# The first two bf16 parts of the second batch's keys: cast on GpSimd instead of ScalarE

## The chip, the cores and the metric

The kernel runs on one core of one Trainium2 chip. The metric is the device time of one execution in microseconds. The core has TensorE (matrix products, written to PSUM), VectorE, ScalarE and GpSimd (elementwise work), and SyncE, on whose queue this kernel issues all its DMAs. The engines run on their own and meet at semaphores only.

## The reference, cut to what matters

The whole reference is two layers of three blocks each (attention over a context, a state-space scan, a low-rank mixture; attention over the context with a mask, attention with compressed and local keys, a mixture of 8 experts), on x of shape (2, 128, 256). The change lies in the first block, and in the work of its second batch:

```
x = x + mha(layernorm(x), ctx, ctx)         # x (2, 128, 256), ctx (2, 2048, 256), 16 heads of 16
scores = einsum('bhqd,bhkd->bhqk', qh, kh) / sqrt(16)
scores = where(ki <= qi + (2048 - 128), scores, -10000)
out = einsum('bhqk,bhkd->bhqd', softmax(scores), vh)
```

Keys and values are the same f32 context. The kernel computes the scores in bf16 with enough parts to come near f32: each key is split into three bf16 parts, part 1 = bf16(K), residue = K - part 1, part 2 = bf16(residue), part 3 = residue - part 2.

## The kernel before, in words

**Groups.** The first block is cut into 8 groups of 4 heads: groups 0 to 3 are batch 0, groups 4 to 7 batch 1. The keys of a group lie in `kS[g % 3]`, 6 x 16 rows of parts (query part times key part) and 2 rows of ones. SyncE fills them with 12 DMAs a group (line 287) out of `ks3[b][part]`, the parts of all keys of batch b. For a group of batch 1 it waits first until `k1_done`, `k2_done` and `k3_done` stand at 6, and before every group from 3 on until the group that used the buffer is over (`pv_done`).

**Passes.** In pass g (g = 0 to 7) two things run beside each other. First, group g is weighed: in 16 chunks of 128 keys TensorE makes the scores plus the bias -max (line 917), ScalarE takes their exponential (line 679), TensorE multiplies by the values (line 930). There are two PSUM buffers of scores, so the scores of chunk c + 2 wait for the exponential of chunk c. Second, TensorE makes the scores of group g + 1 once more (lines 886 to 890), and VectorE reduces them to the maxima of each row in 8 pieces (line 1677). Four tiny VectorE operations behind the eighth (lines 1683 to 1688, semaphore `nm_done`) make the bias of the next group from them: the bias chain. TensorE turns it into rows (line 900), ScalarE copies these (line 579), and the next pass may start. The maxima of group 0 are made ahead of pass 0; `nm_done` stands at g + 2 when the bias chain of pass g is done.

**What ScalarE does beside it.** Other steps are put into ScalarE's order by hand, in the table `beside`: the key (g, c) says that a step runs ahead of the exponential of chunk c in pass g. Among them are `late_part1(j)` and `late_part2(j)` for the 4 heads j of the second batch's K, each one cast of 128x1024, f32 to bf16, and `late_query_rows` (passes 1 and 2), copies of the second batch's queries from PSUM.

**What GpSimd does beside it.** It runs through the groups in order: for each it copies the values into `va[g % 2]` (line 449, semaphore `va_ready`, needed by the first product of values of pass g). For g = 1 it then waits until `nm_done` is 2 (end of pass 0) and makes the residues of the second batch (`late_residue`, line 411, in place in `ctxK`); for g = 2 it waits until `nm_done` is 3 (end of pass 1) and makes part 3 (`late_part3`, line 417). For g = 6 it makes 16 products for the state-space block (lines 437, 425), which begin in pass 5.

**Queries.** `split_queries(1)` on VectorE (lines 1404 to 1408, semaphore `q_split`) splits the queries of the second batch right behind the bias chain of group 0, ahead of the reductions of pass 0.

Of the kernel before, what the change touches and what calls it, by code (L numbers as in the profile page):

```python
# [26 lines left out]
HPG = 4  # L27
# [33 lines left out]
def view(region, start, words, dtype=F32):  # L61
    part = region[:, start:start + words]
    return part if dtype == F32 else part.bitcast(dtype)


def perceiver_program(nc, io, out):
    ctx = ExitStack()
    sems = {}
    with ctx:
# [3 lines left out]
        def S(name):  # L73
            if name not in sems:
                sems[name] = ctx.enter_context(nc.semaphore(name))
            return sems[name]
# [13 lines left out]
        ctxK = reg_a[:, 0:8192].rearrange("p (b j k) -> p b j k", b=NB, j=HPG)  # L90

        part_at = [((reg_b, 12288), (reg_b, 14336), (reg_b, 16384)), ((reg_a, 0), (reg_a, 2048), (reg_b, 18432))]
        ks3 = [[view(r, a, 2048, BF16).rearrange("p (j k) -> p j k", j=HPG) for r, a in ats] for ats in part_at]
# [25 lines left out]
        def weights_of(region, at, gap):  # L119
# [8 lines left out]
               for r, at in ((part_b, 4096), (part_a, 0))]  # L128
# [36 lines left out]
        q_split = [view(oreg, 1024 * b, 768, BF16).rearrange("p (h d t) -> p h t d", h=H0, t=PARTS)  # L165
                   for b in range(NB)]
# [226 lines left out]
        def _(pool):  # L393
            def inv_sqrt(t, b):
                pool.wait_ge(S(f"ln_var{b}"), t + 1)
                pool.tensor_tensor(rstd[b][:, :], var_eps[b][:, :], neg_half, ALU.pow).then_inc(S(f"ln_rstd{b}"), 1)  # L396
# [9 lines left out]
            for i in range(2):  # L406
                pool.wait_ge(S("cleared"), 2)
                pool.memset(va[i][:, :, :, HD0:HD0 + 1], 1.0).then_inc(S("ones_set"), 1)
            def late_residue(j):
                pool.wait_ge(S("k1_done"), 2 + j + 1)  # L410
                pool.tensor_tensor(ctxK[:, 1, j, :], ctxK[:, 1, j, :], ks3[1][0][:, j, :], ALU.subtract)\
                    .then_inc(S("kres_done"), 1)

            def late_part3(j):
                pool.wait_ge(S("kres_done"), 2 + j + 1)
                pool.wait_ge(S("k2_done"), 2 + j + 1)
                pool.tensor_tensor(ks3[1][2][:, j, :], ctxK[:, 1, j, :], ks3[1][1][:, j, :], ALU.subtract)\
                    .then_inc(S("k3_done"), 1)

            def state_input(h):  # L420

                pool.wait_ge(S("dtx_done"), 1)
                pool.wait_ge(S("b_in"), 16)
                for n in range(0, NS, 4):
                    pool.tensor_tensor(state[0][:, h, n:n + 4],
                                       tmp[0][:, h * P:(h + 1) * P].unsqueeze(1).to_broadcast([P, 4, P]),
                                       bc_row[0][:, n:n + 4, :], ALU.mult).then_inc(S("dbx_done"), 1)

            def decay_exponent(h):

                pool.wait_ge(S("ea_done"), 1)
                pool.wait_ge(S("kS_in1"), 16 * REP * 3)
                pool.wait_ge(S("dtx_done"), 1)
                for n in range(0, NS, 4):
                    if (h, n) == (0, 12):
                        pool.wait_ge(S("nm_done"), 6)
                    pool.tensor_tensor(decay[0][:, h, n:n + 4],
                                       dt[0][:, P * h:P * (h + 1)].unsqueeze(1).to_broadcast([P, 4, P]),
                                       ea[:, h, n:n + 4].unsqueeze(2).to_broadcast([P, 4, P]), ALU.mult)\
                        .then_inc(S("dta_done"), 1)  # L440


            for g in range(NG):
                b, hg = divmod(g, NHG)
                pool.wait_ge(S(f"ctxN_in{g % 2}"), 16 * (g // 2 + 1))
                if g >= 2:
                    pool.wait_ge(S("oT_ready"), g - 1)
                src = ctxN[:, b, hg].rearrange("p c (j d) -> p c j d", j=HPG)
                pool.tensor_copy(va[g % 2][:, :, :, 0:HD0], src).then_inc(S("va_ready"), 1)
                if g == 1:  # L450
                    pool.wait_ge(S("nm_done"), 2)
                    for j in range(HPG):
                        late_residue(j)
                if g == 2:
                    pool.wait_ge(S("nm_done"), 3)
                    for j in range(HPG):
                        late_part3(j)
                if g == 5:
                    inv_sqrt(1, 0)
                if g == 6:  # L460
                    decay_exponent(0)
                    decay_exponent(1)
                    state_input(0)
# [63 lines left out]
        def _(sc):  # L527
# [13 lines left out]
            def key_part1(n):  # L541
                b, pair = divmod(n, 2)
                sc.wait_ge(S(f"ctxK_in{n}"), 16)
                sc.copy(ks3[b][0][:, 2 * pair:2 * pair + 2, :], ctxK[:, b, 2 * pair:2 * pair + 2, :])\
                    .then_inc(S("k1_done"), 1)
# [4 lines left out]
                sc.copy(ks3[b][1][:, 2 * pair:2 * pair + 2, :], ctxK[:, b, 2 * pair:2 * pair + 2, :])\  # L550
                    .then_inc(S("k2_done"), 1)

            def late_part1(j):
                sc.wait_ge(S("k3_done"), 2)
                sc.wait_ge(S(f"ctxK_in{2 + j // 2}"), 16)
                sc.copy(ks3[1][0][:, j, :], ctxK[:, 1, j, :]).then_inc(S("k1_done"), 1)

            def late_part2(j):
                sc.wait_ge(S("kres_done"), 2 + j + 1)
                sc.copy(ks3[1][1][:, j, :], ctxK[:, 1, j, :]).then_inc(S("k2_done"), 1)  # L560

            key_part1(0)
            key_part1(1)
            key_part2(0)
# [78 lines left out]
            def state_rates():  # L643
# [2 lines left out]
                sc.activation(ea[:, :, :], ea[:, :, :], ACT.Copy, scale=-1.0).then_inc(S("ea_done"), 1)  # L646


            beside = {(0, 9): [(late_part1, 0)], (0, 11): [(late_part1, 1)], (0, 13): [(late_part1, 2)], (0, 15): [(late_part1, 3)],
                      (1, 7): [(late_part2, 0)], (1, 9): [(late_part2, 1)], (1, 11): [(late_part2, 2)], (1, 13): [(late_part2, 3)],  # L650
                      (1, 8): [(late_query_rows, 0)], (1, 14): [(late_query_rows, 1)], (2, 8): [(late_query_rows, 2)],
                      (2, 13): [(late_query_rows, 3)], (3, 9): [(state_rates,)], (4, 1): [(weigh_masked, 0)], (4, 12): [(transposed_x, 1, 0)],
                      (4, 14): [(copy_z, 0)], (5, 0): [(softplus_exp, 0)], (5, 1): [(softplus_log, 0)], (5, 7): [(copy_maps,)], (6, 1): [(decay_exp, 0, 0)],
                      (6, 5): [(decay_exp, 0, 1)], (6, 9): [(decay_exp, 1, 0)], (6, 13): [(decay_exp, 1, 1)],
# [1274 lines left out]
```

## Time and profile before

| what | value |
|---|---|
| median of 3 runs | 481.57 us (479.76 to 482.05) |
| the profiled execution: its time, its span | 479.39 us, 477.6 us |
| TensorE busy (matmul) | 417.9 us, 87% |
| VectorE busy | 331.0 us, 69% |
| ScalarE busy | 270.2 us, 57% |
| GpSimd busy | 103.5 us, 22% |
| maxima, line 1677, VectorE | 64 x 1221 ns |
| exponentials, line 679, ScalarE | 128 x 598 ns |

The span runs from the first instruction to the last; 1.8 us of the execution's time lie around it. Engines in the rows below are PE (TensorE), PEld (its weight load), DVE (VectorE), ACT (ScalarE), POOL (GpSimd) and SPq (the queue of SyncE). `x2` behind a row means that it merges two instructions; its time is then that of both. Starts are counted from the start of the span. Passes 0 to 7 begin at about 39, 58, 75, 89, 104, 121, 142 and 159 us.

### The profile page before, as it was taken

How to read it: one execution, taken by the hardware profiler on the slowest of the kernel's cores; microseconds unless marked ns; L12 is line 12 of the kernel's file. 1: busy time of each engine (PE TensorE's matmuls, PEld its weight loads, DVE VectorE, ACT ScalarE, POOL GpSimd, SP SyncE). 2: the span in 40 equal slices, each digit the busy share in tenths (PEclk: the TensorE clock that was granted, in tenths of full speed). 3: DMA queues.
4: the chain of work that ended last, by engine and by line, in shares of the span. 5: the costliest groups of instructions: out<-in, count | busy, mean ns of one | idle time of the engine just before them, and what ended most of it. 6: DMA issues, size and time to landing. Idle time of an engine off the chain costs nothing.

```text
span 477.6 us, 9148 instructions
## 1 busy us (share of the span) xinstructions
PE 417.9 (87%) x3661; PEld 308.8 (65%) x3661; DVE 331.0 (69%) x537; ACT 270.2 (57%) x596; POOL 103.5 (22%) x86
## 2 busy tenths in 40 slices
PE   0178799998979898998999999997999799999997
PEld 0125466666646586567543654347999699999996
DVE  3888775769576975987239843874775587787772
ACT  4404888775848834740233724557950566777752
POOL 3002257001078001000003320440020302333300
PEclk9999999999999999999999999999999989999999
DMA  6599185455553054707500000009400884540000
GB/s 232 128 242 298 20 221 151 124 123 145 149 207 86 1 179 132 289 2 301 228 0 0 2 1 0 0 8 355 168 1 2 279 286 149 183 160 2 1 2 22
DMA packets 25003, 58.28 MB, mean 122 GB/s; under 512 B 5210, under 2 KB 13690, under 8 KB 21115
## 3 DMA queue, kind: packets, MB, share of 16 engines
q1 hardware_dynamic: 24960, 57.69, 37.9%
q8 instruction: 29, 0.48, 0.4%
q14 instruction: 14, 0.11, 0.1%
HBM read 44.77 MB, written 0.29 MB: 94 GB/s over the span
## 4 chain that ended last, share of the span: by engine, by line
PE 71%; DVE 14%; ACT 8%; issue 5%; DMA 2%; SPq 0%; POOL 0%; ACTq 0%; DVEq 0%; POOLq 0%
PE ps L1300 19%; PE ps L1101 10%; PE ps L930 7%; PE ps L917 5%; PE ps L886 4%; DVE mx L1677 3%; PE ps L1009 3%; ACT reg_b L679 3%; PE ps L1256 3%; PE ps L965 2%; PE ps L1098 1%; PE ps L1027 1%; PE ps L1246 1%; PE ps L1245 1%; PE ps L1153 1%
## 5 line engine op out<-in xcount | busy, mean ns | idle before, releaser
L1677 DVE TENSOR_REDUCE mx<-ps 128x1 f32<-128x1024 f32 x64 | 77.0, 1221 | 36.6 <-PE ps L886 25.3
L679 ACT ACTIVATE reg_b<-ps 128x512 f32<-128x512 f32 x128 | 75.2, 598 | 28.2 <-PE ps L917 19.8
L917 PE MATMUL ps<-qreg,reg_b 98*128 98x128 bf16 x512 | 46.9, 225 | 5.2 <-ACT reg_b L679 3.8
L1300 PE MATMUL ps<-part_a 128*128 128x256 f32 x384 | 48.2, 283 | 0.4 <-DVE part_a L1834 0.4
L1101 PE MATMUL ps<-reg_b,xT 128*128 128x512 f32 x96 | 47.6, 618 | 0.0
L917 PEld LDWEIGHTS ps<-qreg,reg_b 98*128 98x128 bf16 x512 | 35.5, 100 | 18.5 <-ACT reg_b L679 8.9
L1300 PEld LDWEIGHTS ps<-part_a 128*128 128x128 f32 x384 | 46.9, 192 | 0.6 <-DVE part_a L1834 0.6
L828 ACT ACTIVATE reg_a<-ps,b 128x256 f32<-128x256 f32 x64 | 30.2, 471 | 26.4 <-PE ps L1300 26.4
L930 PE MATMUL ps<-reg_b 128*32 128x128 f32 x1024 | 43.2, 286 | 0.0
L886 PE MATMUL ps<-reg_b,qreg 96*128 96x512 bf16 x96 | 34.1, 424 | 10.3 <-DMA reg_b<-reg_b 7.5
L1834 DVE TENSOR_TENSOR part_a<-reg_a,part_a 128x256 fp32r<-128x256 f32 x64 | 26.9, 436 | 23.2 <-ACT part_a L831 23.2
L1300 PE MATMUL ps<-part_a,part_b 128*128 128x256 f32 x288 | 39.5, 297 | 2.8 <-DVE part_a L1834 2.5
L1300 PEld LDWEIGHTS ps<-part_a,part_b 128*128 128x128 f32 x288 | 37.8, 204 | 3.9 <-issue 2.3
L396 POOL TENSOR_TENSOR rstd<-ve,cf 128x1 f32<-128x1 f32 x12 | 6.7, 560 | 154.2 <-DVE ve L1373 154.2
L688 ACT COPY reg_a<-ps 128x512 f32<-128x512 f32 x24 | 14.0, 586 | 38.8 <-PE ps L1101 38.7
L930 PEld LDWEIGHTS ps<-reg_b 128*32 128x32 f32 x1024 | 25.4, 111 | 6.3 <-issue 0.6
L506 POOL CAST part_b<-reg_b 128x1024 fp32r<-128x1024 f32 (+1 forms) x9 | 15.4, 1723 | 63.6 <-PE ps L1300 29.5
L831 ACT CAST part_a<-reg_a 128x256 fp32r<-128x256 f32 x64 | 26.0, 407 | 2.0
L1101 PEld LDWEIGHTS ps<-reg_b,xT 128*128 128x128 f32 x96 | 16.3, 189 | 16.5 <-issue 16.4
L886 PEld LDWEIGHTS ps<-reg_b,qreg 96*128 96x128 bf16 x96 | 8.0, 100 | 22.3 <-DVE mx L1677 8.0
L538 ACT COPY xT<-ps 128x256 f32<-128x256 f32 x10 | 3.7, 374 | 32.6 <-PE ps L852 32.6
L1780 DVE TENSOR_TENSOR part_a<-reg_b,part_a 128x1024 fp32r<-128x1024 f32 (+1 forms) x12 | 20.8, 1743 | 0.8 <-ACT part_a L839 0.8
(279 smaller groups left out, 857.0 us busy)
## 6 DMA issues: line engine op xcount, KB each, us to landing
reg_b<-in_w SPq DMA_DIRECT2D x16, 512.0 KB, 8.5
reg_b<-in_w SPq DMA_DIRECT2D x8, 1024.0 KB, 7.8
reg_b<-reg_b SPq DMA_DIRECT2D x56, 128.0 KB, 3.5
reg_b<-in_w_qkv SPq DMA_DIRECT2D x3, 2048.0 KB, 7.4
reg_b<-reg_a SPq DMA_DIRECT2D x40, 128.0 KB, 3.1
reg_a<-in_ctxK SPq DMA_DIRECT2D x4, 1024.0 KB, 7.0
reg_a<-in_ctx SPq DMA_DIRECT2D x8, 512.0 KB, 5.0
reg_b<-bc_mem SPq DMA_DIRECT2D x4, 1024.0 KB, 5.6
```

Of the source, the lines that this page charges most:

```text
L506: pool.tensor_copy(high[e % 2][i], raw[e % RAW][i]).then_inc(S(name), 1)
L679: sc.activation(pT[n % 3], score_b[n % 2], ACT.Exp).then_inc(S("exp_done"), 1)
L828: sc.activation(hid[layer][:, m, :], ps[:, 2 + m, 0:NB * P], ACT.Gelu, bias=(b1, b2)[layer][:, e, m:m + 1]).then_inc(S(f"h{layer + 1}_sb"), 1)
L831: sc.copy(hid_high[layer][:, m, :], hid[layer][:, m, :]).then_inc(S(f"h{layer + 1}_high"), 1)
L886: mm = pe.matmul(score_a[m % 2][:, i, :], q, k, start=True, stop=True)
L917: mm = pe.matmul(cols, kS[g % 3][0:SROWS, c // 8, j, P * (c % 8):P * (c % 8 + 1)], qT[b][0:SROWS, HPG * hg + j, :], start=not last, stop=True)
L930: mm = pe.matmul(ps[VW * j:VW * (j + 1), 7, 0:P], va[g % 2][:, c, j, :], pT[n % 3][:, P * j:P * (j + 1)], start=c == 0, stop=c == NCH - 1)
L1101: mm = pe.matmul(bank(b, n % 2), xT[b][:, i, :], w_qkv[j][:, i, 512 * n:512 * (n + 1)], start=False, stop=i == KD - 1)
L1300: mm = pe.matmul(out, left[u], right[v], start=(i, u, v) == (0, 0, 0), stop=(i, u, v) == (len(terms) - 1, 0, 1))
L1677: ve.reduce_max(mx[:, piece // 2, piece % 2:piece % 2 + 1], score_a[m % 2].rearrange("p i k -> p (i k)"), X_AXIS).then_inc(S("max_done"), 1)
L1780: ve.tensor_tensor(low[e % 2][i], raw[e % RAW][i], high[e % 2][i], ALU.subtract).then_inc(S("w_low"), 1)
L1834: ve.tensor_tensor(hid_low[layer][:, m, :], hid[layer][:, m, :], hid_high[layer][:, m, :], ALU.subtract).then_inc(S(f"h{layer + 1}_low"), 1)
```

## The change

The two helpers move from ScalarE's program to GpSimd's. Their eight entries in `beside` go away. On GpSimd, part 1 of all four heads stands ahead of the copy of group 1's values, behind a new wait for `q_split` = 2, the end of `split_queries(1)`. Part 2 of all four heads stands behind the four residues, and so ahead of the copy of group 2's values. Semaphores, shapes and buffers stay as they were; `sc.copy` becomes `pool.tensor_copy`.

```diff
--- before.py
+++ after.py
@@ -406,6 +406,15 @@
             for i in range(2):
                 pool.wait_ge(S("cleared"), 2)
                 pool.memset(va[i][:, :, :, HD0:HD0 + 1], 1.0).then_inc(S("ones_set"), 1)
+            def late_part1(j):
+                pool.wait_ge(S("k3_done"), 2)
+                pool.wait_ge(S(f"ctxK_in{2 + j // 2}"), 16)
+                pool.tensor_copy(ks3[1][0][:, j, :], ctxK[:, 1, j, :]).then_inc(S("k1_done"), 1)
+
+            def late_part2(j):
+                pool.wait_ge(S("kres_done"), 2 + j + 1)
+                pool.tensor_copy(ks3[1][1][:, j, :], ctxK[:, 1, j, :]).then_inc(S("k2_done"), 1)
+
             def late_residue(j):
                 pool.wait_ge(S("k1_done"), 2 + j + 1)
                 pool.tensor_tensor(ctxK[:, 1, j, :], ctxK[:, 1, j, :], ks3[1][0][:, j, :], ALU.subtract)\
@@ -445,12 +454,18 @@
                 pool.wait_ge(S(f"ctxN_in{g % 2}"), 16 * (g // 2 + 1))
                 if g >= 2:
                     pool.wait_ge(S("oT_ready"), g - 1)
+                if g == 1:
+                    pool.wait_ge(S("q_split"), 2)
+                    for j in range(HPG):
+                        late_part1(j)
                 src = ctxN[:, b, hg].rearrange("p c (j d) -> p c j d", j=HPG)
                 pool.tensor_copy(va[g % 2][:, :, :, 0:HD0], src).then_inc(S("va_ready"), 1)
                 if g == 1:
                     pool.wait_ge(S("nm_done"), 2)
                     for j in range(HPG):
                         late_residue(j)
+                    for j in range(HPG):
+                        late_part2(j)
                 if g == 2:
                     pool.wait_ge(S("nm_done"), 3)
                     for j in range(HPG):
@@ -550,15 +565,6 @@
                 sc.copy(ks3[b][1][:, 2 * pair:2 * pair + 2, :], ctxK[:, b, 2 * pair:2 * pair + 2, :])\
                     .then_inc(S("k2_done"), 1)
 
-            def late_part1(j):
-                sc.wait_ge(S("k3_done"), 2)
-                sc.wait_ge(S(f"ctxK_in{2 + j // 2}"), 16)
-                sc.copy(ks3[1][0][:, j, :], ctxK[:, 1, j, :]).then_inc(S("k1_done"), 1)
-
-            def late_part2(j):
-                sc.wait_ge(S("kres_done"), 2 + j + 1)
-                sc.copy(ks3[1][1][:, j, :], ctxK[:, 1, j, :]).then_inc(S("k2_done"), 1)
-
             key_part1(0)
             key_part1(1)
             key_part2(0)
@@ -646,9 +652,7 @@
                 sc.activation(ea[:, :, :], ea[:, :, :], ACT.Copy, scale=-1.0).then_inc(S("ea_done"), 1)
 
 
-            beside = {(0, 9): [(late_part1, 0)], (0, 11): [(late_part1, 1)], (0, 13): [(late_part1, 2)], (0, 15): [(late_part1, 3)],
-                      (1, 7): [(late_part2, 0)], (1, 9): [(late_part2, 1)], (1, 11): [(late_part2, 2)], (1, 13): [(late_part2, 3)],
-                      (1, 8): [(late_query_rows, 0)], (1, 14): [(late_query_rows, 1)], (2, 8): [(late_query_rows, 2)],
+            beside = {(1, 8): [(late_query_rows, 0)], (1, 14): [(late_query_rows, 1)], (2, 8): [(late_query_rows, 2)],
                       (2, 13): [(late_query_rows, 3)], (3, 9): [(state_rates,)], (4, 1): [(weigh_masked, 0)], (4, 12): [(transposed_x, 1, 0)],
                       (4, 14): [(copy_z, 0)], (5, 0): [(softplus_exp, 0)], (5, 1): [(softplus_log, 0)], (5, 7): [(copy_maps,)], (6, 1): [(decay_exp, 0, 0)],
                       (6, 5): [(decay_exp, 0, 1)], (6, 9): [(decay_exp, 1, 0)], (6, 13): [(decay_exp, 1, 1)],
```

## Rows read from the trace of the kernel before

**Rows 1.** The page of the run, the chain that ended last, by engine.
```profile
PE 71%; DVE 14%; ACT 8%; issue 5%; DMA 2%; SPq 0%; POOL 0%; ACTq 0%; DVEq 0%; POOLq 0%
```

**Rows 2.** The chain of waits, 30 to 92 us: start us, us, what.
```profile
48.52 0.58 issue
...
53.23 2.37 DVE mx L1677 x2
...
66.92 0.67 issue
...
71.22 0.52 issue
```

**Rows 3.** Timeline of ScalarE: start us, us, engine, line, operation, [idle before <- releaser].
```profile
57.52 1.20 ACT L679 ACTIVATE reg_b<-ps 128x512 f32<-128x512 f32 x2
...
64.28 1.04 ACT L560 CAST reg_a<-reg_a 128x1024 bf16<-128x1024 f32 x1
...
72.22 0.58 ACT L573 COPY qreg<-ps 96x512 bf16<-96x512 bf16 x1
...
73.98 1.20 ACT L679 ACTIVATE reg_b<-ps 128x512 f32<-128x512 f32 x2
...
86.21 0.57 ACT L573 COPY qreg<-ps 96x512 bf16<-96x512 bf16 x1
...
88.92 1.20 ACT L679 ACTIVATE reg_b<-ps 128x512 f32<-128x512 f32 x2
```

**Rows 4.** Timeline of VectorE, passes 0 to 2 and pass 5.
```profile
38.40 1.01 DVE L1404 TENSOR_SCALAR tmp<-xn 128x256 f32<-128x256 f32 x1
...
48.86 2.36 DVE L1677 TENSOR_REDUCE mx<-ps 128x1 f32<-128x1024 f32 x2 [0.40 <-PE ps L890]
...
56.28 0.17 DVE L1688 TENSOR_TENSOR nm<-negm,nm 128x4 bf16<-128x4 f32 x1
...
69.86 1.23 DVE L1677 TENSOR_REDUCE mx<-ps 128x1 f32<-128x1024 f32 x1 [0.25 <-PE ps L890]
...
83.21 3.48 DVE L1677 TENSOR_REDUCE mx<-ps 128x1 f32<-128x1024 f32 x3 [0.39 <-PE ps L890]
...
87.40 0.17 DVE L1688 TENSOR_TENSOR nm<-negm,nm 128x4 bf16<-128x4 f32 x1
...
136.68 0.80 DVE L1683 TENSOR_TENSOR m<-mx 128x4 f32<-128x4 f32 x1
...
139.51 0.96 DVE L1688 TENSOR_TENSOR nm<-negm,nm 128x4 bf16<-128x4 f32 x1
```

**Rows 5.** Timeline of TensorE, the bias turned into rows at the end of passes 1 and 2.
```profile
72.96 0.33 PE L900 MATMUL ps<-cb,nm 128*2 128x128 bf16 x3
...
87.90 0.33 PE L900 MATMUL ps<-cb,nm 128*2 128x128 bf16 x3
```

**Rows 6.** Timeline of GpSimd, whole run.
```profile
37.19 2.08 POOL L449 COPY reg_b<-reg_a 128x1024 f32<-128x1024 f32 x2
56.53 8.40 POOL L411 TENSOR_TENSOR reg_a<-reg_a 128x1024 f32<-128x1024 f32 x4 [17.26 <-DVE nm L1688]
...
72.03 8.40 POOL L417 TENSOR_TENSOR reg_b<-reg_a 128x1024 bf16<-128x1024 f32 x4 [5.79 <-DVE nm L1688]
...
134.43 8.02 POOL L437 TENSOR_TENSOR reg_a<-tmpb,ea 128x512 f32<-128x512 f32 x8 [6.02 <-DMA reg_b<-reg_b]
...
373.58 2.02 POOL L506 CAST part_a<-reg_b 128x1024 fp32r<-128x1024 f32 x2 [2.35 <-DVE part_a L1808]
```

**Rows 7.** Timeline of the DMA queue, loads of group 3 and the last of group 4.
```profile
59.59 7.52 SPq L287 DMA_DIRECT2D reg_b<-reg_b  x12
...
83.48 1.22 SPq L287 DMA_DIRECT2D reg_b<-reg_b  x2
```

**Rows 8.** The page, DMA issues: count, KB each, median us to landing.
```profile
reg_b<-reg_b SPq DMA_DIRECT2D x56, 128.0 KB, 3.5
```

**Rows 9.** Windows at the start of pass 6: stretch, its us, TensorE busy (instructions), granted clock, DMA share, GB/s.
```profile
142.00:144.00 2.00, 2.00 (x22) 0.50 0.00 0
```

## The prediction

> **What bounds the kernel now.** I read the chain of waits of the whole run first, then the chain between 30 and 92 us alone, then the timelines of ScalarE, VectorE, GpSimd, TensorE and the DMA queue over the same stretch. Passes are counted as in the text above: pass g weighs group g and takes the maxima of group g + 1.
>
> The chain of the whole run gives 71% to TensorE, 14% to VectorE and only 8% to ScalarE [rows 1]. So taking 8 us of ScalarE work away is worth what ScalarE holds up, not 8 us. Within passes 0 and 1 it does hold something up. ScalarE's casts come in the middle of its exponentials, and each exponential behind a cast makes TensorE wait before the next chunk of scores. The chain shows such waits, as "issue", ahead of an exponential: 0.58 us at 48.52 in pass 0, 0.67 us at 66.92 and 0.52 us at 71.22 in pass 1 [rows 2]. The reader should also see where pass 0 ends: the last piece before the end of the maxima is VectorE's, two reductions from 53.23, 2.37 us. Pass 0 is handed from ScalarE to VectorE.
>
> How long a pass is without casts is seen next door. A mark of a pass is the exponential right behind the copy of the bias rows (that of chunk 15, the first of two at 57.52, 73.98 and 88.92). From mark to mark pass 1 takes 73.98 - 57.52 = 16.46 us; pass 2, with the same schedule of matmuls and reductions and also two copies of query rows, but no cast, takes 88.92 - 73.98 = 14.94 us [rows 3].
>
> **The change part by part.**
>
> *ScalarE, eight casts gone.* Four lie in pass 1, 1.04 us each as the one at 64.28 [rows 3], and four of the same shape in pass 0: 8.3 us busy.
>
> Pass 0: in the trace VectorE finishes its fifth reduction of the pass at 48.86 + 2.36 = 51.22 [rows 4], then runs the last three with gaps, ending at 53.23 + 2.37 = 55.60 [rows 2]. Without the casts before exponentials 9 and 11, TensorE is about 0.9 us earlier with the scores of those pieces (the 0.58 us wait of [rows 2] and a smaller one behind it). Then VectorE is late next and runs back to back: 51.22 + 3 x 1.18 = 54.8. Saved: 0.8 us. The casts beside chunks 13 and 15 are worth nothing, VectorE covers them.
>
> Pass 1: it becomes like pass 2, which is worth 16.46 - 14.94 = 1.52 us. The waits named above, 0.67 + 0.52, make most of it. In which half it comes: from its mark to the end of the last reduction pass 1 takes 69.86 + 1.23 - 57.52 = 13.57 us, pass 2 takes 83.21 + 3.48 - 73.98 = 12.71 us [rows 3, 4]; so 0.86 us ahead of the short chain of VectorE that makes the bias, 0.66 us behind it. A little more is to be had behind it. In pass 2 TensorE turns the bias into rows at 87.90, although VectorE had it at 87.40 + 0.17 = 87.57 [rows 4, 5]: ScalarE's copy of query rows at 86.21 lay before exponential 13, for which TensorE waits. In pass 1 that copy lies one chunk later (72.22, behind exponential 13) [rows 3], so TensorE can start 0.04 us behind VectorE: 0.3 us more. In all 0.8 + 1.5 + 0.3 = 2.6 us.
>
> *GpSimd, four part-1 casts and the wait for `q_split`.* No row of this kernel shows a GpSimd cast from f32 to bf16. From below: its cast of 128x1024 f32 to fp32r takes 2.02 us for two, so 0.98 us each behind one another and 1.04 us for the last; its copy of the same size takes 1.04 us [rows 6]. From above: the two-input subtraction that writes bf16, 8.40 us for four, 2.1 us each. The subtraction with an f32 result costs the same 8.40 us [rows 6], so writing bf16 costs nothing there, and what doubles the price is the second input. I take 1.0 us. Part 1 then runs from the end of the split of Q at about 43 to 47, and the copy of V for group 1 queued behind it ends at 48. The earliest user of that copy runs after 57.52, so either end of the price is hidden. Nobody else waits on GpSimd in between. The copy of V no longer lies beside the split of Q, whose first step took 1.01 us at 38.40 beside a GpSimd copy [rows 4, 6]; that gives VectorE up to 0.7 us, worth nothing, since TensorE is the next to be late there.
>
> *GpSimd, four part-2 casts in pass 1.* This is the step that can hurt. GpSimd starts its residues when the bias chain of pass 0 ends, T = 56.28 + 0.17 = 56.45, at 56.53, and is through at 64.93 [rows 4, 6]; what is queued behind is now part 2 (4.0 us) and then the V copy for group 2 (1.04 us), which ends at T + 0.08 + 8.35 + 4.0 + 1.04 = T + 13.5. The bias chain of pass 1 starts at the end of the last reduction, T + 1.07 (the mark, 57.52) + 12.71 = T + 13.8. What happens when the two meet is in the trace, in pass 5: while GpSimd runs 8 subtractions on end from 134.43, the four tiny VectorE operations take from 136.68 to 139.51 + 0.96 = 140.47, 3.8 us [rows 4, 6], against 83.21 + 3.48 = 86.69 to 87.57, 0.9 us, in pass 2. So the new GpSimd work clears VectorE's chain by some 0.3 us. The reductions themselves, which read PSUM, are not touched: 1.23 us in pass 1.
>
> The Trainium skill ("SBUF — State Buffer", Who interferes with whom) has the rule for this: VectorE and GpSimd share a port pair as an exclusive lock, held for the whole instruction, which a VectorE operation with two SBUF inputs or in a two-port mode wants and `tensor_reduce` never does. The trace agrees (0.9 against 3.8 us). The rule speaks against this change just so far as the two stretches overlap, which is the rival below. The same skill ("GPSIMD Engine Reference", Engine selection) calls one-input work on GpSimd roughly line-rate and two-input work about twice as slow; by it the casts are the 1.0 us that the rows give.
>
> *Part 3 and the DMA queue.* Part 3 waits for the bias chain of pass 1 on GpSimd, 72.03 before and about 70.2 after, when part 2 and the V copy are over; it takes 8.40 us to 78.6. The queue wants it for the last two loads of group 4, at 83.48 before, 80.9 after [rows 7]: 2 us of slack. The wait for part 1 and part 2 ends 2 us and more ahead of the first of these loads. The loads of group 3 start at the end of pass 0, so they move by 0.8 us only, while their first use, behind the row at 72.96, moves by 2.3: the last is issued at 59.59 + 7.52 = 67.1, lands some 3.5 us later, at 70.6, and 70.6 - 0.8 is still ahead of 72.96 - 2.0 [rows 5, 7, 8]. V copies in time for group 2: needed after 71.4, there at 69.2. Everything from pass 2 on hangs on semaphores of the passes before it and slides along whole.
>
> **The sum.** 479.39 us of the profiled execution - 2.6 = 476.8. That execution lies 2.2 us under the median of the runs shown (481.57), and the prediction goes by that median: 479.0 us.
>
> **The rivals.**
>
> *R1, a brush with VectorE's chain.* If a bf16 cast takes 0.1 us more than 1.0, or gaps between the instructions add up to 0.3 us, the V copy for group 2 reaches into the bias chain of pass 1. For it: a margin of 0.3 us over 13 us. Against: at most one copy (1.04 us) is in the way, since GpSimd then waits. It costs 0.1 to 1.0 us, 0.6 in the middle: 479.6 us.
>
> *R2, the slow cast: slower than before.* If bf16 output costs GpSimd 2.1 us, part 2 runs to T + 16.8 and the copy to T + 17.9. The point from which it decides is a GpSimd that is still casting at T + 13.8. Each of the first three small VectorE operations then waits for one GpSimd instruction, as in pass 5, and the chain ends at about T + 18.2 with T = 55.65, so at 73.85 instead of 71.96. TensorE gets to the row of 72.96 at 73.9, 0.9 us late, after an idle time of over 3 us; after such a time, at the start of pass 6, the granted clock stood at 0.50 from 142 to 144, the lower level of 1.2 GHz [rows 9], which costs at least 1.0 us there, some 1.5 with its edges. Sum +2.4: 484.0 us. Against it: the bf16 and f32 results of equal price [rows 6].
>
> *R3, hidden anyway or given back.* The saving is met by another limit: VectorE's reductions in pass 1, a load that lands late in pass 3, or the long collision of pass 5 falling out 1 or 2 us worse, since it hangs on a DMA landing. For it: VectorE has 14% of the chain, and three reductions back to back at the end of pass 2 [rows 4]. Against: pass 2 shows that the same work fits into 14.94 us. 481.5 us.
>
> **How the numbers follow.** Forecast 0.60, R1 0.17, R2 0.10, R3 0.13. A measurement of this kernel tells a change from none from about 0.5%, 2.4 us, on; the forecast of 2.6 lies almost on that line. Half and a little more of the forecast counts as faster (0.33), a quarter of R1 (0.04) and some room for a gain larger than thought (0.03): 0.40. Slower: two thirds of R2 and a little of R3, 0.09. The rest, 0.51, is within the line. The forecast alone reaches from 477.6 to 480.4 (0.5 us on each term of the sum, and the spread of medians); with R1, R3 and part of R2 the range is 477.3 to 482.2.
>
> **What would show it.** Passes 0 and 1 without a ScalarE cast, the last reduction of pass 0 ending at 54.8, the marks at 56.7, 71.4 and 86.3; GpSimd casts of 1.0 us; VectorE's bias chain in pass 1 still 0.9 us long and GpSimd idle before it; the DMA queue never waiting for part 3. The prediction is wrong if pass 1 is longer than 15 us, if the chain in pass 1 takes over 1 us, if the casts take 2 us, or if pass 5 differs from before by over 0.5 us.

## The result, and the profile after

The changed kernel takes 478.06 us, median of 14 runs (474.8 to 482.87); the kernel before takes 480.68 us in the 14 runs beside them (479.07 to 484.62). The ratio is 0.9932, with a 95% interval from 0.9907 to 0.9958: 3.3 us faster, between 2.0 and 4.5. The forecast was 479.0 us and 2.6 us faster. The ratio leaves out the run of 482.87 us, which is over 1.5% above the fastest. It is not the quotient of the two medians, which differ by 2.6 us. Every "us faster" below is worked out from a ratio. The profiled execution of the changed kernel took 477.84 us, span 476.1 us. Line numbers have moved: the reductions are line 1681 now, the bias chain 1687 to 1692 and the exponentials 683 (4 higher than before), ScalarE's copies of query rows 579 and of bias rows 585 (6 higher).

The chain that ended last, from the page, answers to [rows 1]:

```profile
PE 72%; DVE 13%; ACT 7%; issue 4%; DMA 2%; SPq 0%; POOL 0%; ACTq 0%; DVEq 0%; POOLq 0%
```

ScalarE went from 8% to 7% and VectorE from 14% to 13%. Where the time came from is seen in ScalarE's timeline, which answers to [rows 3]. The marks of the passes are the first of the two exponentials:

```profile
55.92 1.20 ACT L683 ACTIVATE reg_b<-ps 128x512 f32<-128x512 f32 x2
...
68.82 0.57 ACT L579 COPY qreg<-ps 96x512 bf16<-96x512 bf16 x1
...
70.63 1.20 ACT L683 ACTIVATE reg_b<-ps 128x512 f32<-128x512 f32 x2
...
85.57 1.20 ACT L683 ACTIVATE reg_b<-ps 128x512 f32<-128x512 f32 x2
...
138.59 0.60 ACT L683 ACTIVATE reg_b<-ps 128x512 f32<-128x512 f32 x1
```

Before, the marks stood at 57.52, 73.98 and 88.92; now they stand at 55.92, 70.63 and 85.57, so 1.60, 3.35 and 3.35 us earlier. Pass 1 takes 70.63 - 55.92 = 14.71 us where it took 16.46, and pass 2 takes 14.94 us in both. The copy of query rows at 68.82 lies behind exponential 13, and most of the 0.3 us that were to come from this did come: pass 1 is 0.23 us shorter than pass 2. The last row, the first exponential of pass 6, stood at 141.59 before and stands 3.0 us earlier now.

VectorE's timeline, answering to [rows 4] (start us, us):

```profile
38.44 0.29 DVE L1408 TENSOR_SCALAR tmp<-xn 128x256 f32<-128x256 f32 x1
...
46.38 1.23 DVE L1681 TENSOR_REDUCE mx<-ps 128x1 f32<-128x1024 f32 x1 [0.34 <-PE ps L890]
48.00 5.97 DVE L1681 TENSOR_REDUCE mx<-ps 128x1 f32<-128x1024 f32 x5 [0.40 <-PE ps L894]
54.01 0.16 DVE L1687 TENSOR_TENSOR m<-mx 128x4 f32<-128x4 f32 x1
...
65.15 3.49 DVE L1681 TENSOR_REDUCE mx<-ps 128x1 f32<-128x1024 f32 x3 [0.40 <-PE ps L894]
68.67 0.16 DVE L1687 TENSOR_TENSOR m<-mx 128x4 f32<-128x4 f32 x1
...
69.34 0.17 DVE L1692 TENSOR_TENSOR nm<-negm,nm 128x4 bf16<-128x4 f32 x1
...
133.47 0.80 DVE L1687 TENSOR_TENSOR m<-mx 128x4 f32<-128x4 f32 x1
...
136.31 0.96 DVE L1692 TENSOR_TENSOR nm<-negm,nm 128x4 bf16<-128x4 f32 x1
```

In pass 0 five reductions run back to back from 48.00 and end at 53.97, where 54.8 was forecast. In pass 1 the last one ends at 65.15 + 3.49 = 68.64, and the bias chain behind it (68.67 to 69.51) is 0.84 us long as ever. In pass 5 the collision with GpSimd's products is as it was: 133.47 to 137.27, 3.8 us. The first step of the split of Q at 38.44 takes 0.29 us where it took 1.01.

The third reduction of pass 0 (46.38) and the first operation of the bias chain (54.01) measure what the casts cost in pass 0 without what varies ahead of them. In the trace of before these two were:

```profile
47.24 1.23 DVE L1677 TENSOR_REDUCE mx<-ps 128x1 f32<-128x1024 f32 x1 [0.34 <-PE ps L886]
...
55.62 0.16 DVE L1683 TENSOR_TENSOR m<-mx 128x4 f32<-128x4 f32 x1
```

From the one to the other it took 55.62 - 47.24 = 8.38 us; now it takes 54.01 - 46.38 = 7.63 us, 0.75 less. The other 0.9 us by which pass 0 is shorter in this trace come ahead of the third reduction.

GpSimd's timeline, answering to [rows 6]:

```profile
43.02 4.00 POOL L412 CAST reg_a<-reg_a 128x1024 bf16<-128x1024 f32 x4 [4.76 <-DVE oreg L1412]
46.97 1.04 POOL L462 COPY reg_b<-reg_a 128x1024 f32<-128x1024 f32 x1
54.92 8.40 POOL L420 TENSOR_TENSOR reg_a<-reg_a 128x1024 f32<-128x1024 f32 x4 [6.91 <-DVE nm L1692]
63.27 3.99 POOL L416 CAST reg_a<-reg_a 128x1024 bf16<-128x1024 f32 x4
67.21 1.04 POOL L462 COPY reg_b<-reg_a 128x1024 f32<-128x1024 f32 x1
69.59 8.41 POOL L426 TENSOR_TENSOR reg_b<-reg_a 128x1024 bf16<-128x1024 f32 x4 [1.34 <-DVE nm L1692]
```

Four casts to bf16 take 4.00 us. They cost what casts to fp32r cost, 0.98 us each. The copy of V for group 2 ends at 67.21 + 1.04 = 68.25, and VectorE's chain starts at 68.67: it is cleared by 0.4 us, where 0.3 were forecast.

What the passes gained did not all arrive at the end: 3.35 us at the end of pass 2, 1.5 us in the span. The granted clock says where the rest went. The columns are the stretch, its us, TensorE busy, granted clock, DMA share and GB/s:

```profile
226.00:228.00 2.00, 2.00 (x13) 0.58 0.00 0
137.00:139.00 2.00, 1.63 (x21) 0.50 0.00 0
139.00:141.00 2.00, 2.00 (x21) 0.50 0.00 0
```

The stretch at the lower level (0.50, 1.2 GHz) at the start of pass 6 costs 2.5 us here, against 1.7 us in the trace of before (TensorE's busy time times what is missing of the clock, over windows of 1 us). One from 224 to 228 costs 1.7 us and has no counterpart before. Neither stands at a place that the change touches. In the two further traces of the same kernel below, the stretch at the start of pass 6 comes again and costs 3.1 and 1.7 us, and the one near 226 does not come at all.

### The profile page after: what moved, and what is told of

The parts are those of the page before. It is cut to its first block, busy times and chain, and to the rows that moved or that the text cites. A ratio compares the mean times of both kernels' runs of the same rounds, so it can differ in the third digit from the quotient of the medians.

```text
span 476.1 us, 9149 instructions
## 1 busy us (share of the span) xinstructions
PE 418.5 (88%) x3661; PEld 310.1 (65%) x3661; DVE 330.9 (70%) x537; ACT 263.9 (55%) x588; POOL 111.4 (23%) x94
## 4 chain that ended last, share of the span: by engine, by line
PE 72%; DVE 13%; ACT 7%; issue 4%; DMA 2%; SPq 0%; POOL 0%; ACTq 0%; DVEq 0%; POOLq 0%
PE ps L1304 19%; PE ps L1105 10%; PE ps L934 6%; PE ps L921 5%; PE ps L890 4%; DVE mx L1681 4%; PE ps L1013 3%; PE ps L1260 3%; PE ps L969 3%; ACT reg_b L683 3%; PE ps L1039 2%; PE ps L1102 1%; PE ps L1031 1%; PE ps L1250 1%; PE ps L1249 1%
## 5 line engine op out<-in xcount | busy, mean ns | idle before, releaser
L921 PE MATMUL ps<-qreg,reg_b 98*128 98x128 bf16 x512 | 45.9, 225 | 4.1 <-ACT reg_b L683 2.8
L921 PEld LDWEIGHTS ps<-qreg,reg_b 98*128 98x128 bf16 x512 | 35.4, 100 | 16.5 <-ACT reg_b L683 7.1
L1105 PEld LDWEIGHTS ps<-reg_b,xT 128*128 128x128 f32 x96 | 16.3, 189 | 16.5 <-issue 16.4
```

What stands on the lines that cost most here:

```text
L921: mm = pe.matmul(cols, kS[g % 3][0:SROWS, c // 8, j, P * (c % 8):P * (c % 8 + 1)], qT[b][0:SROWS, HPG * hg + j, :], start=not last, stop=True)
L1105: mm = pe.matmul(bank(b, n % 2), xT[b][:, i, :], w_qkv[j][:, i, 512 * n:512 * (n + 1)], start=False, stop=i == KD - 1)
```

## The experiments

Ratios are against the kernel before, timed on the same chip beside each group of runs. There are three groups, each on another chip: the first three variants with the changed kernel's second trace, the next four, and the last three with its third trace. Pass lengths are from one copy of the bias rows to the next.

**Part 1 alone, part 2 alone.** In the first, `late_part2` is back on ScalarE with its four entries; in the second, `late_part1` is, and GpSimd's wait for `q_split` is gone.

```diff
 # part 1 only
-                    for j in range(HPG):
-                        late_part2(j)
+            beside = {(1, 7): [(late_part2, 0)], (1, 9): [(late_part2, 1)], ...
```

> Only part 1 goes to GpSimd; part 2 stays on ScalarE in pass 1. Theory A (ScalarE's casts held TensorE up in both passes, independently): pass 0 ends as in the changed kernel, mark at about 56 instead of 57.5, pass 1 stays at 16.4 us from mark to mark: 1.6 us faster than before (0.8 us if the earlier rise of TensorE's pace in pass 0 was luck of that execution). Rival B (the gain hangs on pass 1 alone): pass 0 unchanged, no gain.

> Only part 2 goes to GpSimd; part 1 stays on ScalarE in pass 0, and the V copy of group 1 stays beside the split of Q. Theory A: pass 0 ends with the mark at 57.5 as before, pass 1 takes 14.7 us: 1.8 us faster than before. Rival B (the two edits lean on each other, since GpSimd's work starts at the end of pass 0): pass 1 is longer than 15 us.

Measured: 0.9971 (0.9935 to 1.0007) and 0.9963 (0.9928 to 0.9999), that is 1.4 and 1.8 us; each alone is close to what a measurement can tell. Their sum, 3.2 us, agrees with the 3.3 us of both together, but the intervals (each nearly 2 us to either side) would allow much else. ScalarE's copies of the bias rows, part 1 alone:

```profile
38.35 0.57 ACT L587 COPY qreg<-ps 2x512 bf16<-2x512 bf16 x1 [16.65 <-PE ps L907]
...
56.66 0.57 ACT L587 COPY qreg<-ps 2x512 bf16<-2x512 bf16 x1 [2.45 <-PE ps L907]
...
75.54 0.57 ACT L587 COPY qreg<-ps 2x512 bf16<-2x512 bf16 x1
```

and part 2 alone:

```profile
38.21 0.57 ACT L586 COPY qreg<-ps 2x512 bf16<-2x512 bf16 x1 [16.68 <-PE ps L906]
...
56.55 0.57 ACT L586 COPY qreg<-ps 2x512 bf16<-2x512 bf16 x1 [1.46 <-PE ps L906]
...
72.77 0.57 ACT L586 COPY qreg<-ps 2x512 bf16<-2x512 bf16 x1
```

Pass 0 is 18.31 us in the first, against 19.08 in the trace of before, but it is 18.34 in the second too, where the casts of part 1 are back and 19.1, as before, was expected. The whole length of pass 0 therefore settles nothing. The measure from the third reduction to the bias chain does: 7.63 us in the first, 8.38 in the second.

Pass 1 was expected at 16.4 and 14.7 and came out at 18.88 and 16.22. In both the granted clock stood at 0.50 at its start (55 to 63 us and 57 to 62 us), which took 3.2 and 1.7 us from TensorE. What such stretches add to pass 1 is seen in the other traces: those that took 3.2 us from TensorE have a pass 1 of 17.1 us instead of 14.7, those that took 1.7 have 16.0. Less these 2.4 and 1.3 us, the two passes are 16.5 and 14.9 us. So each edit works on its own pass, as far as one trace of each with such a correction can tell.

**The V copy alone.** To the kernel before, only the wait for the split of Q was added ahead of GpSimd's V copy of group 1.

```diff
+                if g == 1:
+                    pool.wait_ge(S("q_split"), 2)
                 src = ctxN[:, b, hg].rearrange("p c (j d) -> p c j d", j=HPG)
```

> The kernel before, with GpSimd's V copy of group 1 put behind the split of Q and nothing else. Theory C (the 0.8 us of pass 0 that the prediction had not counted come from VectorE, whose split of Q no longer waits for that copy, so that TensorE gets its fast pace earlier): the second reduction of pass 0 starts at 44.8 instead of 45.7 and the mark comes 0.3 to 0.8 us earlier. Rival D (the moment of the faster pace differs from execution to execution, or hangs on the casts): the split is 0.7 us shorter, the second reduction and the mark stay at 45.7 and 57.5; no gain.

Measured: 0.9989 (0.9949 to 1.0029). VectorE's timeline has the split 0.7 us shorter and the second reduction where it was:

```profile
38.45 0.29 DVE L1406 TENSOR_SCALAR tmp<-xn 128x256 f32<-128x256 f32 x1
...
45.62 1.23 DVE L1679 TENSOR_REDUCE mx<-ps 128x1 f32<-128x1024 f32 x1 [1.46 <-PE ps L892]
```

Passes 0 and 1 take 18.98 and 16.45 us, as before. Theory C falls in this trace: VectorE's freed time brings the mark no earlier, as the prediction had it. The timing alone (between 2.5 us faster and 1.4 slower) could not tell.

**The changed kernel again, twice.**

> The changed kernel once more, as the yardstick of this chip and for a second trace. If the pace of pass 0 rises at 43.5 us again, it belongs to the kernel; if at 44.6 us, to the execution. The stretches of lower granted clock that the first trace of it had at 137 to 142 and at 220 to 230 us should lie elsewhere or be of another length if they are luck. Time 0.7% under before.

> The changed kernel a third time, to measure the variants of this call against it on this chip, and for a third trace of it. Theory E: pass 1 is 14.7 us in the trace if no stretch at half of the clock falls into it, 16 to 17 us if one does. 0.3 to 0.8% under before.

Measured: 0.9964 (0.9924 to 1.0004) and 0.9935 (0.9901 to 0.9969). With the result's 0.9932 these are 3.3, 1.7 and 3.1 us. Now the question of pass 0. TensorE's timeline in the first trace has the values' matmuls at full pace from 43.54 (16 in 0.65 us):

```profile
43.54 0.65 PE L934 MATMUL ps<-reg_b 128*32 128x128 f32 x16
```

In the second trace of the same kernel they still take 1.08 us at 43.43 and are fast from 46.63 on:

```profile
43.43 1.08 PE L934 MATMUL ps<-reg_b 128*32 128x128 f32 x16
...
46.63 0.64 PE L934 MATMUL ps<-reg_b 128*32 128x128 f32 x15
```

The granted-clock column says 1.00 in both, so the row with the pace has to be read and not that column. Pass 0 took 17.44, 18.94 and 18.23 us in the three traces. In the eight traces of these experiments and of the result in which part 1 left ScalarE and nothing else differs in pass 0, it took 17.4 to 18.9 us, 18.3 in the middle; in the three with the casts 19.08, 18.98 and 18.34. The two groups overlap, so the whole length cannot measure the casts. From the third reduction to the bias chain it can: 8.38 us in all three traces with the casts, and 7.62 or 7.63 us in all eleven without. That is 0.75 us for the casts; everything else in which the traces differ lies ahead of the third reduction. The 0.8 us beyond the forecast were luck of that execution.

The third trace shows the other thing that varies, at the start of pass 1:

```profile
56.00:58.00 2.00, 2.00 (x22) 0.50 0.02 4
58.00:60.00 2.00, 2.00 (x25) 0.50 0.00 0
```

There pass 1 took 17.09 us instead of 14.71. Without part 1 on ScalarE the lower clock fell into the start of pass 1 in seven of nine traces (until the matmuls below were added), with it in one of three. These are too few to say that the change brings it. Averaged over whole runs, the granted clock of the changed kernel was 0.979 (12 runs) against 0.981 before (35 runs) on one chip and 0.981 (12) against 0.983 (23) on another: the same direction, and small.

**More work on GpSimd in pass 1.** One, then four casts more, each beside one of part 2.

```diff
 # four more; the run with one more has the same two lines for j = 0 only
                     for j in range(HPG):
+                        pool.wait_ge(S('kres_done'), 2 + j + 1)
+                        pool.tensor_copy(ks3[1][2][:, j, :], ctxK[:, 1, j, :])
                         late_part2(j)
```

> The changed kernel with one more GpSimd cast of the same size ahead of part 2 in pass 1 (it writes into the place of part 3, which is overwritten later). In the changed kernel GpSimd ends 0.42 us ahead of VectorE's bias chain in pass 1; 0.99 us more make it end 0.57 us behind the chain's start. Theory A (exclusive: an operation of the chain waits for the GpSimd instruction that is running): the first operation of the chain takes 0.6 to 0.7 us instead of 0.16, the other three are as short as before; pass 1 is 0.3 to 0.6 us longer than 14.7. Rival (the two only slow each other by a share): all four a little longer.

> The changed kernel with four more GpSimd casts in pass 1, one beside each of part 2, so that part 2 costs what rival R2 of the prediction gave it, 8 us. R2's mechanism: each of the four operations of the bias chain waits for one GpSimd instruction, about 1 us each; the chain takes 3.4 to 3.8 us instead of 0.9, pass 1 takes 17.0 to 17.6 us instead of 14.7, TensorE sits idle 3 us or more ahead of pass 2 and has a stretch at 0.50 behind it: 3 to 5 us slower than the changed kernel, equal to the kernel before or slower. Rival (GpSimd casts are out of the way of everything): pass 1 stays at 14.7.

The single extra cast decided nothing. In its trace the lower clock made pass 1 17.13 us long, VectorE's chain started at 72.42, and GpSimd had been through since 70.33; all four operations were short. The four extra casts gave 1.0029 (1.0003 to 1.0055), 1.4 us slower than before. VectorE's chain of pass 1 there:

```profile
71.23 0.34 DVE L1689 TENSOR_TENSOR m<-mx 128x4 f32<-128x4 f32 x1
71.61 0.96 DVE L1691 TENSOR_SCALAR negm<-m,cf 128x4 f32<-128x4 f32 x1
72.61 0.95 DVE L1693 CAST nm<-negm 128x4 bf16<-128x4 f32 x1
73.60 0.17 DVE L1694 TENSOR_TENSOR nm<-negm,nm 128x4 bf16<-128x4 f32 x1
```

The chain takes 2.54 us instead of 0.84. Three of its operations waited, the fourth found GpSimd through (its V copy ended at 73.53). That is less than the 3.4 us expected, since the lower clock had put VectorE 1 us later, but it is the mechanism of rival R2, and with it the gain is gone: slower than before by 1.4 us (0.1 to 2.6), where R2 had 2.4. The stretch at the lower clock that R2 put behind it did not come in this trace.

**Without the wait for the split of Q.**

```diff
-                    pool.wait_ge(S("q_split"), 2)
```

> The changed kernel without the wait for the split of Q ahead of part 1: the casts start at 38.3 us, beside the split. Theory A: each step of the split waits for a cast, the split ends at 44 to 46 instead of 42.9, the first reduction of pass 0 with it; VectorE catches up only in part, and pass 0 is 0.5 to 1.5 us longer. Rival (the wait is not needed, TensorE is late in that stretch anyway): the split is longer but the mark of pass 1 stays; no difference beyond 0.3 us.

Measured: 0.9947 (0.9925 to 0.9969), no difference from the changed kernel that can be told. The collision is there:

```profile
43.82 1.82 DVE L1411 TENSOR_TENSOR oreg<-tmpb,oreg 128x256 bf16<-128x256 f32 x1
45.36 2.30 DVE L1680 TENSOR_REDUCE mx<-ps 128x1 f32<-128x1024 f32 x2
```

The casts began at 40.01 and not at 38.3 as expected (the trace has them wait for a DMA), so they met only the later steps of the split. It ends at 45.64 instead of 42.90, and the first reduction starts 2.4 us later (0.5 us of both because this whole trace is later from the start). But VectorE catches up: its last reduction of pass 0 ended at 55.95, pass 0 took 18.88 us. The rival held, by and large: pass 0 lies within what it takes in the changed kernel (17.4 to 18.9 us). A worth of the wait of a few tenths, or even 1 us, is not excluded, since the changed kernel was not timed in this group.

**The collision of pass 5.** All 16 products behind the bias chain of pass 5; then only the fourth and later.

```diff
 # all
+                pool.wait_ge(S("nm_done"), 7)
                 pool.wait_ge(S("ea_done"), 1)
 # from the fourth
                     if (h, n) == (0, 12):
-                        pool.wait_ge(S("nm_done"), 6)
+                        pool.wait_ge(S("nm_done"), 7)
```

> The changed kernel, with GpSimd's 16 products of the state-space block waiting until the bias chain of pass 5 is over (one more wait, nm_done = 7, nothing else). Theory A (the same collision costs the kernel 3 us in pass 5, and the wait behind it brings the lower clock at the start of pass 6): the chain of pass 5 takes 0.9 us instead of 3.8, TensorE's idle time there shrinks from 3.7 to under 1.5 us, the stretch at 0.50 at the start of pass 6 is gone: 3 to 5 us faster than the changed kernel, some 6 us faster than the kernel before. Rival (the products are then late): ScalarE waits for them in pass 6 or VectorE's scan does in pass 7, and the gain is under 1 us.

> The changed kernel, with only the fourth and later of GpSimd's products waiting for the bias chain of pass 5 (nm_done = 7 where it waited for 6). Three products fit ahead of the chain, the rest behind it. Theory A (a collision costs what it overlaps, and the run before moved all of it from pass 5 into the chain of pass 6): the chain of pass 5 takes 1 to 2 us instead of 3.8, the chain of pass 6 is met by the last product or two only, at most 2 us instead of 4.5; passes 5 and 6 together are 2 us shorter than in the changed kernel, 1 to 3 us faster than it. Rival (the products need more room than a pass has, however they are cut): the sum of both chains stays at 4.7 us or more, no gain.

All of them late: 0.9942 (0.9913 to 0.9971), no gain over the changed kernel that can be told (0.9932, 0.9964 and 0.9935 in its own three measurements). Theory A and its rival were both wrong about where: ScalarE and the scan waited for nothing, but the collision moved on by one pass. VectorE's first operation of the chain in pass 5 and in pass 6:

```profile
137.14 0.16 DVE L1688 TENSOR_TENSOR m<-mx 128x4 f32<-128x4 f32 x1
...
152.98 3.94 DVE L1688 TENSOR_TENSOR m<-mx 128x4 f32<-128x4 f32 x1
```

and GpSimd's products:

```profile
138.06 8.03 POOL L447 TENSOR_TENSOR reg_a<-tmpb,ea 128x512 f32<-128x512 f32 x8 [9.20 <-DVE nm L1693]
...
150.96 1.03 POOL L463 COPY reg_b<-reg_a 128x1024 f32<-128x1024 f32 x1
151.96 4.94 POOL L434 TENSOR_TENSOR reg_a<-tmp,reg_b 128x512 f32<-128x512 f32 x4
```

The chain of pass 6 began inside the last four products and waited until all four were over, 3.94 us at one operation. The stretch at the lower clock moved along, from the start of pass 6 to the start of pass 7 (157 to 162). From the fourth on: 0.9883 (0.9835 to 0.9930), 5.6 us faster than before and 2.5 us faster than the changed kernel timed beside it (0.9935); the two intervals still overlap a little, and there are 6 runs. The same two operations there:

```profile
134.68 0.53 DVE L1687 TENSOR_TENSOR m<-mx 128x4 f32<-128x4 f32 x1
...
150.89 0.95 DVE L1687 TENSOR_TENSOR m<-mx 128x4 f32<-128x4 f32 x1
```

0.53 and 0.95 us are left of a collision of 3.8; the chain of pass 5 is 1.2 us long, that of pass 6 1.6. Passes 5 and 6 take 35.1 us together, against 38.4 in the changed kernel's trace of this group.

**TensorE kept busy at the end of pass 0.**

```diff
                             misc_read(*read_before_rows[g + 1])
+                        if g == 0:
+                            keep_busy(6, 14)
                         max_to_rows(g + 1)
```

> The changed kernel with 14 matmuls of constants at the end of pass 0, about 1.7 us, where TensorE waits 2.0 us for VectorE's bias chain (their result is not used). Theory E (the stretch at half of the clock that most traces without casts in pass 0 show at the start of pass 1 follows that idle time, and eats 1.6 to 3.2 us of the gain): granted clock 1.00 from 54 to 64, pass 1 at 14.7 us in the trace, and 1 to 2 us faster than the changed kernel. Rival (that stretch comes whatever TensorE does there): it is still there, no difference.

> Both edits of the two runs above in one kernel. Theory A and E together: the sum of the two gains, 2 to 5 us faster than the changed kernel, 5 to 8 us faster than the kernel before. If either falls, only the other one's share.

Alone: 0.9911 (0.9875 to 0.9946), 4.3 us faster than before and 1 us faster than the changed kernel timed beside it; the intervals overlap. The clock stays up:

```profile
54.00:56.00 2.00, 1.87 (x20) 1.00 0.00 0
56.00:58.00 2.00, 1.58 (x26) 1.00 0.01 4
```

Pass 1 took 14.71 us here and 14.70 with both edits: 0 of 2 traces with the lower clock, against 7 of 9. The clock averaged over whole runs agrees: 0.986 with the matmuls against 0.981 in the changed kernel (12 runs each), and 0.993 with both edits against 0.986 with the products split (6 runs each). With both edits: 0.9829 (0.9781 to 0.9877), 471.69 us against 481.49, 8.2 us faster than before and 5.1 us faster than the changed kernel (0.9935). It is the fastest version that was run, with 6 runs. ScalarE's copies of the bias rows in it:

```profile
38.20 0.57 ACT L585 COPY qreg<-ps 2x512 bf16<-2x512 bf16 x1 [16.71 <-PE ps L904]
...
56.24 0.57 ACT L585 COPY qreg<-ps 2x512 bf16<-2x512 bf16 x1 [2.25 <-PE ps L904]
...
70.94 0.57 ACT L585 COPY qreg<-ps 2x512 bf16<-2x512 bf16 x1
...
135.39 0.57 ACT L585 COPY qreg<-ps 2x512 bf16<-2x512 bf16 x1 [0.91 <-PE ps L904]
...
151.97 0.57 ACT L585 COPY qreg<-ps 2x512 bf16<-2x512 bf16 x1 [0.62 <-PE ps L904]
```

Pass 0 18.04, pass 1 14.70, pass 5 18.18 (before 21.07), pass 6 16.58 (before 17.49) us. Between the first and the last of the copies passes 0 to 6 are 6.9 us shorter than in the trace of before, and the whole span is 8.4 us shorter. The rest goes with the lower clock behind pass 6: while TensorE works it comes once in this trace, from 372 to 377, where the trace of before has it at 189 to 192 and at 379 to 387 as well as at the start of pass 6. No edit touches those places, and no run shows why it stayed away there, so 1.5 us of the 8 are not shown to belong to the edits.

## Why the prediction was right

- **ScalarE's casts in pass 1: 1.8 us.** Measured 1.75 (16.46 to 14.71). To read the pass next door, which does the same without the casts, gave this to 0.1 us. Four traces without a stretch at the lower clock have 14.70 or 14.71 us, the two with the casts have 16.45. The copy of query rows behind exponential 13 gave 0.23 of its 0.3 us: TensorE starts on the bias rows 0.10 us behind VectorE (69.61 against 69.51) and not 0.04.
- **Pass 0: 0.8 us.** 1.6 in the first trace, of which the casts are 0.75: from the third reduction to the bias chain 8.38 us in three traces with them and 7.63 in eleven without. VectorE became the limit, as forecast: its five reductions end back to back. The rest, 0.9 us, was luck: the moment at which TensorE's pace nearly doubled, by 43.5 us in the first trace of this kernel and by 46.6 in the second.
- **The price of a GpSimd cast to bf16: 1.0 us.** 4.00 us for four. The upper bound, 2.1 us, was the price of two inputs.
- **VectorE's chain cleared by 0.3 us.** 0.4 us, and the chain 0.84 us long. Rivals R1 and R2 did not occur; that R2's mechanism works was shown with four extra casts.
- **Part 3 and the DMA queue.** Part 3 started at 69.59 and was through at 78.00, ahead of the loads that want it, issued from 79.73 on. Pass 2 kept its 14.94 us. Nothing came late.
- **R3, given back elsewhere.** Pass 5 is 0.44 us longer than before in the first trace (21.51 against 21.07), just inside the 0.5 us that the prediction allowed; in the two further traces it is 0.1 us longer and 0.2 shorter. What the first trace gave back behind pass 2 goes for the most part with the clock.
- **The time of 479.0 us.** It was taken from a median of 3 runs, 481.57; in 14 runs the kernel before has 480.68. So the time forecast is 0.9 us above the measured one for a reason that has nothing to do with the change. The marks (55.92, 70.63 and 85.57 for 56.7, 71.4 and 86.3) and the end of pass 0's last reduction (53.97 for 54.8) are all early by the 0.8 us of luck in pass 0. The prediction also calls GpSimd's work of pass 5 subtractions; they are products, with no effect on the sum.
- **What the prediction did not have.** It took the clock at the start of pass 1 for granted. TensorE gets there at the lower level in most traces without casts in pass 0. That takes 1.6 to 3.2 us of TensorE's time and makes pass 1 1.2 to 2.4 us longer, which stands against the 2.6 us in part of the executions. It was named for pass 6 only, inside R2. By the prediction's own sign, a pass 1 of over 15 us, two of the three traces of the changed kernel (15.95 and 17.09 us) would have called it wrong; what makes them longer is the lower clock and not the casts. The spread of the runs goes with the granted clock of the whole run (474.8 us at 0.993 and 482.87 at 0.972), but not with this place alone: the kernel before spreads as much (476.95 us at 0.992 and 484.29 at 0.972 in 35 runs). That the sum still met the mean does not say that every execution gains 2.6 us. Whether the stretch really comes more often without casts in pass 0, and why, stays open: TensorE's idle time ahead of it is 2.0 us in the changed kernel and 2.1 before, in traces with and without it. That the clock stays up behind the 14 matmuls in this idle time was seen in two traces, and two of the nine without them had it too; that it is the source of their gain is likely and not beyond the intervals.

## What to carry to other kernels

To price work taken out of a loop, look for an iteration of the same loop that already runs without it, and compare from mark to mark; the engine's busy time is a poor guide (8.3 us of ScalarE's were taken away here, for 3.3 us). When work goes to GpSimd, list the VectorE operations on the path that read or write SBUF and check, in us, that GpSimd is silent while they run; reductions out of PSUM don't count (1.23 us here with GpSimd's casts beside them and without). Where such a series must cross a short serial chain, cutting it there so that most of it waits is worth a try (2.5 us here). So are idle matmuls in a link in which TensorE waits 2 us for another engine; here they gave 1 us alone, within the noise, and 2.6 us on top of the cut series, part of it at places that they do not touch. And where traces of one kernel differ, look for a stretch between two marks that is equal in all of them, and measure the change there.

## What the runs showed of the hardware

- How long VectorE waits differs with GpSimd's instructions. Against casts and against the products of line 446, whose operands are both small ones read over and over, each small operation that waited in full got in after one GpSimd instruction, 0.95 to 0.97 us each (0.16 to 0.23 alone). Against the products of line 434, whose second operand is a large one, one operation waited at 152.98 for the rest of a series of four, 3.94 us. This was seen once; the other meetings with that line fell into the last product of the series.
- The same place of the program runs at 2.4 GHz in one execution and at 1.2 GHz in another. On one chip, the changed kernel had a pass 1 of 17.09 us with the granted clock at 0.50, and the kernel with the products split, which is the same up to pass 5, had 14.70 us at 1.00. All 14 traces agree within 0.04 us in the length of pass 2 and of pass 3. In pass 1, three traces of one and the same kernel (not all on one chip) have 14.71, 15.95 and 17.09 us.
